# Roots from ScalarE's logarithm and exponential, and GpSimd's digit products in two halves of the tokens, in an audio tower kernel

## The chip, the cores and the metric

One core of a Trainium2 chip runs the whole kernel. The metric is the device time of one execution in microseconds (us), as the median of several runs. PE is the matmul engine, DVE the vector engine, ACT the scalar engine, POOL GpSimd, SP the queue that issues the transfers.

## The reference

The input is 32 clips of 40,000 samples. Cut to what matters:

```python
frames = pad(x).reshape(32, 313, 128)
h = einsum('bfh,kh->bfk', frames, dct_basis)             # 313 tokens of 128 per clip
n = layernorm(h)                                         # (h - mean) / sqrt(var + 1e-5)
h = h + softmax(n @ n.T) @ n                             # attention within a clip
n = layernorm(h)
q = layernorm((n @ Wq.T + bq) per head of 64) * ln_g + ln_b   # 8 heads
s0, s1 = l2norm(q[:32]) @ l2norm(keys0).T, l2norm(q[32:]) @ l2norm(keys1).T
top 16 of s0 and of s1, top 16 of their 256 sums, softmax -> w, expert index fi
h = h + sum over heads and picks of gelu(n . expert_down[fi]) * w * expert_up[fi]
```

Four roots stand in it: one for each layernorm over a token (1 and 2), one for the layernorm of each head (3), and one for the norm of each half of a head (4). A fifth, for the norm of the keys, is taken once.

## The kernel before

Two clips make a pair; there are 16 pairs. The 626 tokens of a pair are cut into five tiles of 128 tokens, so there are 80 tiles. The kernel has no loop on the device: every engine's program is written out, in an order that the function `drive` gives and that is the same for all of them.

`drive` cuts the time of a tile into four steps p = 0 to 3 (a slot is (pair k, tile t, step p)). In a slot each engine does the work of several tiles, each in another stage: scores and the top 16 of tile n, candidates of tile n-1, softmax weights of n-2, digits and products (`hi`, `lo`, `alpha`, `beta`, `bw`) of n-3, the small matmuls ("quads", `QB<-bw,alpha`) of n-4, the output of n-5. Between these slots stands the front of the next pair, `front(k + 1, t, p)`: transform and first squares in slot 0, attention in slots 0 and 1, second squares and `hid` in slot 2, head projections and their squares in slots 2 and 3, the head roots at (3,3), their transposes and the scores of the next pair in slot 4. Each engine works through its own list in order, and waits at a semaphore where its list asks for it; so one late instruction holds everything behind it on its engine.

The roots were made in two parts. DVE made a seed from the bits of the number (`seed`, L928 and L929; for the two row roots L980 brings the mean square first), and POOL made three Newton steps of four instructions each (`newton`, L780). Root 1 of the next pair: seed in DVE's slot 0, step 2, inside the list of `max_index` instructions, Newton at POOL's front (0,2), used by ACT's `xns` (L627) there. Root 2: seed at DVE's front (2,1), Newton at POOL's front (2,0), used by ACT's `hid` (L654) at (2,1). Root 3: seed at DVE's front (3,3), Newton and then a chain for `std` and `stdin` on POOL, transposed by PE at (4,0) and copied by ACT (`stdT`, L679). Root 4: seed by `norms` in DVE's slot 0, step 2, Newton at the head of POOL's slot (1,0).

POOL's products `bw` of a tile are three instructions (L914), each the product of `beta` with one of three parts of `wp`, for all 32 tokens of each group of the layout. PE's four steps of quads take the tokens 8 at a time: step p reads columns 8p to 8p+7. All four wait, by the wait at p = 0, for the whole of `bw`.

Per pair ACT calls Gelu once (slot 4, L719) and Exp many times: for `E` (L640, attention), `zexp` (L689) and `wexp` (L693). All its other functions are Copy, Identity, Square and Relu.

Of the kernel before, what the change touches and what calls it, by code (L numbers as in the profile page):

```python
# [9 lines left out]
I32 = mybir.dt.int32  # L10
# [28 lines left out]
RSQRT_MAGIC = float(0x5F3759DF)  # L39
# [41 lines left out]
def build(nc, x, Wq, bq, ln_g, ln_b, keys0, keys1, down, up, ident_d, dct_d, indc_d, sel_d, row8_d, sel3_d, out):  # L81
# [4 lines left out]
    with ctx:  # L86
# [6 lines left out]
        def sem(name):  # L93
# [12 lines left out]
        c15 = sb("c15", [128, 80])  # L106
# [55 lines left out]
        y4 = sb("y4", [128, 80])  # L162
# [75 lines left out]
            kseed_full knewton kn_full kbT_full dT_full weights_ready x_full xT_copied ss1_full sv1 seed1_full  # L238
            newton1 xn_full xnT_copied e_full rden_full h2c_full ss2_full sv2 seed2_full newton2 h2_full
            hid_full hidTn_full sq_full v3_full seed3_full newton3 std_full stdT_full hidT_full  # L240
# [5 lines left out]
            wb_steps stat_full vt_full std_steps nrm_steps n2_steps seed4_full""".split()  # L246
# [128 lines left out]
        def _(pe):  # L375
# [119 lines left out]
            def slot(k, t, p):  # L495
# [87 lines left out]
        def _(act):  # L583
# [14 lines left out]

            def squares(dst, src, over, b, done):


                for c, (st, n) in enumerate(CH):
                    last = A(over[0:n, b, c, 0:D], src(c, n), ACT.Square, accum_out=dst[0:n, 3 * b + c:3 * b + c + 1])
                last.then_inc(done, 1)
                return last

            def front(j, t, p):
# [14 lines left out]
                if (t, p) == (0, 2):  # L622
                    act.wait_ge(s["newton1"], 12 * j + 12)
# [26 lines left out]
                if (t, p) == (2, 1):  # L650
                    act.wait_ge(s["newton2"], 12 * j + 12)
# [15 lines left out]
                if (t, p) in ((2, 3), (3, 1)):  # L667
# [3 lines left out]
                    A(statT[:, NF * b:NF * b + NF], bank[0:40, 0:NF], ACT.Copy).then_inc(s["vt_full"], 1)  # L671
                if (t, p) == (4, 0):
# [10 lines left out]
            def slot(k, t, p):  # L683
# [10 lines left out]
                if p == 0 and exists(k, t, 3):  # L694
                    buf = RING[(t - 3) % NT]
                    act.wait_ge(s["st_full"], n - 2)
                    after(act, s["bw_full"], n - 4)
# [54 lines left out]
            def late(t, p):  # L752
                if (t, p) == (1, 3):
                    setup()
# [15 lines left out]
        def _(pool):  # L770
            tt = nc.gpsimd.tensor_tensor

            def newton(y, xh, a, c, sem_, base, end=None):

                i = 0
                for r in range(3):
                    for o, p0, p1, op in ((a, y, y, ALU.mult), (a, a, xh, ALU.mult), (a, a, c, ALU.add), (end if end is not None and r == 2 else y, y, a, ALU.mult)):
                        if i:
                            pool.wait_ge(sem_, base + i)
                        tt(o, p0, p1, op).then_inc(sem_, 1)  # L780
                        i += 1

            def setup():
# [3 lines left out]
                nc.gpsimd.memset(c15[:], 1.5)  # L787
# [13 lines left out]
            def late(t, p):  # L801
                if (t, p) == (0, 1):
                    pool.wait_ge(s["kseed_full"], 1)
                    newton(ky[:], kxh[:], ka[:], c15[0:64, 0:2], s["knewton"], 0)

            def front(j, t, p):
                if (t, p) == (0, 2):
                    pool.wait_ge(s["seed1_full"], j + 1)
                    newton(sy[0][:], sxh[0][:], sa[:, 0:6], c15[:, 0:6], s["newton1"], 12 * j)
                if (t, p) == (2, 0):  # L810
                    pool.wait_ge(s["seed2_full"], j + 1)
                    newton(sy[1][:], sxh[1][:], sa[:, 0:6], c15[:, 0:6], s["newton2"], 12 * j)
                if (t, p) == (3, 3):
                    pool.wait_ge(s["seed3_full"], j + 1)
                    newton(y3[:], xh3[:], sa[:], c15[:, 0:40], s["newton3"], 12 * j)
                    pool.wait_ge(s["newton3"], 12 * j + 12)
# [22 lines left out]
            def half_norms(j):  # L839
# [6 lines left out]

                tt(halves(nB[:]), halves(nB[:]), both(std[:]), ALU.mult).then_inc(s["nrm_steps"], 1)
# [18 lines left out]
            def slot(k, t, p):  # L866
# [10 lines left out]
                if p == 0 and t == 1 and exists(k, t, 0):  # L877
                    pool.wait_ge(s["seed4_full"], k + 1)
                    newton(y4[:], xh4[:], na[:], c15[:], s["rn_steps"], 12 * k, rn[:])
                if p == 0 and exists(k, t, 1):  # L880
# [3 lines left out]
                    pool.wait_ge(s["rn_steps"], 12 * kk + 12)  # L884
# [23 lines left out]
                if p == 3 and exists(k, t, 3):  # L908
# [14 lines left out]
        def _(dve):  # L923
            V = nc.vector

            def seed(x_, xh, y, done):

                V.tensor_scalar(xh, x_, -0.5, None, ALU.mult)  # L928
                V.tensor_scalar(y.bitcast(I32), x_.bitcast(I32), -0.5, RSQRT_MAGIC, ALU.mult, ALU.add).then_inc(done, 1)  # L929

# [3 lines left out]
            def setup():  # L934
# [8 lines left out]
                dve.wait_ge(s["kss_part"], 3)  # L943
                seed(kss[:], kxh[:], ky[:], s["kseed_full"])
# [258 lines left out]
```

## Time and profile before

| | |
|---|---|
| median of 3 runs | 2025.39 us (2025.3 to 2026.98) |
| the profiled execution | 2031.43 us, its span 2029.6 us |
| mean granted PE clock | 0.812 |
| busy in the span: PE, DVE, ACT, POOL | 1632.5, 1919.0, 1232.0, 1433.2 us |
| first and last tile begin on DVE (first L1062 of the tile) | 82.0 and 1945.0 us |

The rows further down come from the trace of the profiled execution. A row of a timeline says when a group of like instructions began, how long it took, what it wrote and read, and in square brackets how long the engine had been idle before it and what ended that. A row of the groups gives the busy time in all and the mean of one in ns. DMA plays no part: its queues are nearly empty.

### The profile page before, as it was taken

To read this page: it belongs to the slowest core of one execution; us is meant where nothing else is said; L and a number is where in the kernel's file an instruction comes from. 1 tells how busy PE (TensorE), PEld (TensorE's weight loads), DVE (VectorE), ACT (ScalarE), POOL (GpSimd) and SP (SyncE) were. 2 spreads that over 40 slices of the span, in tenths; PEclk is the share of its full clock that TensorE was granted. 3 is DMA by queue.
4 is the path that set the end of the run, shared out by engine and by line. 5 is a ranking of instruction groups with operands and counts; after the bars stand their busy time and mean duration, and the time that the engine had idled before them with its cause. 6 is when DMAs were issued, how large, how long until landed. Compare 5 with 4: busy or idle time off the path is not lost.

```text
span 2029.6 us, 47236 instructions
## 1 busy us (share of the span) xinstructions
PE 1632.5 (80%) x11023; PEld 1169.5 (58%) x11023; DVE 1919.0 (95%) x15718; ACT 1232.0 (61%) x3883; POOL 1433.2 (71%) x2561
## 2 busy tenths in 40 slices
PE   5577888788888888888888788888878888986667
PEld 3235566566656655665666556656656565655456
DVE  2499999999999999999999999999999999999992
ACT  3346666666666666566556766656675665665554
POOL 2247777686777767777776777777687777767775
PEclk8877888888888787888888787888888888788765
DMA  1000000000000000000000000000000000000000
GB/s 44 7 10 4 19 7 13 13 7 19 7 19 9 13 13 6 19 7 19 7 6 22 6 19 7 19 7 7 19 9 20 7 19 7 6 13 9 7 6 11
DMA packets 46669, 24.87 MB, mean 12 GB/s; under 512 B 4827, under 2 KB 46116, under 8 KB 46390
## 3 DMA queue, kind: packets, MB, share of 16 engines
q1 hardware_dynamic: 46390, 21.85, 3.9%
q8 instruction: 89, 1.46, 0.3%
q14 instruction: 190, 1.56, 0.3%
HBM read 11.58 MB, written 10.26 MB: 11 GB/s over the span
## 4 chain that ended last, share of the span: by engine, by line
DVE 79%; PE 11%; ACT 5%; issue 4%; POOL 1%; SPq 1%; DMA 0%; DVEq 0%; ACTq 0%
DVE idx L1071 11%; DVE idx L1078 11%; DVE hrest L1065 10%; DVE alpha L1039 10%; DVE vals L1069 7%; DVE vals L1062 7%; DVE c L1109 5%; DVE crest L1103 5%; DVE top L1106 3%; DVE top L1100 3%; PE QB L526 2%; DVE beta L1044 2%; PE FB L418 1%; PE QB L514 1%; DVE lo L1033 1%
## 5 line engine op out<-in xcount | busy, mean ns | idle before, releaser
L914 POOL TENSOR_TENSOR bw<-beta,wp 128x1024 bf16<-128x1024 bf16 x240 | 505.2, 2135 | 347.3 <-issue 171.6
L526 PE MATMUL QB<-bw,alpha 128*128 128x48 bf16 x5120 | 554.5, 277 | 106.7 <-issue 101.1
L526 PEld LDWEIGHTS QB<-bw,alpha 128*128 128x128 bf16 x5120 | 521.0, 150 | 149.2 <-issue 139.4
L749 ACT ACTIVATE WD<-QB 32x96 f32<-32x96 f32 x1280 | 307.6, 240 | 84.5 <-PE QB L526 71.6
L1039 DVE TENSOR_SCALAR alpha<-hi 128x1024 bf16<-128x1024 bf16 x640 | 274.9, 502 | 0.0
L475 PE MATMUL SC<-WK,hidT 128*128 128x512 f32 x320 | 241.0, 846 | 12.6 <-issue 11.8
L1071 DVE FIND_INDEX8 idx<-vals,sraw 128x8 uint32<-128x64 f32 x1280 | 250.6, 218 | 0.0
L1078 DVE FIND_INDEX8 idx<-vals,hrest 128x8 uint32<-128x64 f32 x1280 | 250.6, 219 | 0.0
L1065 DVE MATCH_REPLACE8 hrest<-vals,sraw 128x64 f32<-128x64 f32 x1280 | 249.6, 207 | 0.0
L1062 DVE MAX8 vals<-sraw 128x8 f32<-128x64 f32 x1280 | 169.1, 207 | 14.1 <-ACT sraw L729 14.1
L1069 DVE MAX8 vals<-hrest 128x8 f32<-128x64 f32 x1280 | 166.6, 208 | 0.0
L729 ACT ACTIVATE sraw<-SC 128x1024 f32<-128x1024 f32 x80 | 83.3, 1041 | 115.5 <-PE SC L476 114.8
L429 PE MATMUL FB<-hidTn,WcT 128*128 128x313 f32 x256 | 113.6, 594 | 49.2 <-ACT sq L665 37.2
L862 POOL TENSOR_TENSOR ci<-idxf 128x64 f32<-128x64 f32 (+3 forms) x400 | 126.2, 362 | 12.6 <-ACT idxf L710 12.5
L862 POOL TENSOR_TENSOR cs<-vs 128x64 f32<-128x64 f32 (+3 forms) x400 | 125.1, 350 | 6.3
L475 PEld LDWEIGHTS SC<-WK,hidT 128*128 128x128 f32 x320 | 79.8, 270 | 82.4 <-issue 76.1
L715 ACT ACTIVATE hi<-EB,cdig 128x256 bf16<-128x256 f32 x320 | 124.3, 473 | 0.0
L1109 DVE MATCH_REPLACE8 c<-top,crest 128x54 f32<-128x54 f32 x640 | 122.6, 243 | 0.0
L1103 DVE MATCH_REPLACE8 crest<-top,cs 128x54 f32<-128x54 f32 x640 | 118.8, 198 | 0.0
L493 PE MATMUL U<-wp,minusb 128*128 128x256 bf16 x160 | 51.2, 320 | 82.2 <-ACT wp L732 82.2
L514 PE MATMUL QB<-upR,Gd 128*128 128x128 f32 x640 | 112.2, 331 | 4.5 <-issue 4.2
L906 POOL TENSOR_TENSOR Yw<-wz,m 128x432 f32<-128x432 f32 x80 | 107.5, 1344 | 6.3
(206 smaller groups left out, 3583.3 us busy)
## 6 DMA issues: line engine op xcount, KB each, us to landing
res<-h_scratch SPq DMA_DIRECT2D x80, 64.0 KB, 1.9
xin<-in_x SPq DMA_DIRECT2D x32, 128.0 KB
h_scratch<-h2n SPq DMA_DIRECT2D x32, 128.0 KB
out<-ofin SPq DMA_DIRECT2D x64, 64.0 KB, 1.5
h_scratch<-h2n SPq DMA_DIRECT2D x32, 28.5 KB
out<-ofin SPq DMA_DIRECT2D x16, 57.0 KB
xin<-in_x SPq DMA_DIRECT2D x32, 28.0 KB
xin<-in_x SPq DMA_DIRECT2D x32, 0.2 KB
```

The lines of the kernel that those rows point to most:

```text
L475: mm(SC[:, cols], hidT[:, t1, :], WK[:, cols], start=True, stop=False)
L526: last = mm(bank[:, 48 * u:48 * u + 48], alpha[:, buf, a, :, 8 * p + u], bwv[:, :, a, :, 8 * p + u], start=(a == 0), stop=(a == 1))
L749: last = A(WD[r, RING[(t - 4) % NT], :, 8 * p:8 * p + 8], blocks[r, :, :, g], ACT.Copy)
L862: last = tt(o, a0, a1, ALU.add)
L914: last = tt(bw[:, buf, NY * i:NY * i + NY, :], beta[:, buf, :, :], wp[:, buf, i, :].unsqueeze(1).to_broadcast([128, NY, 256]), ALU.mult)
L1039: last = V.tensor_scalar(a8[:, :, :, xx, :], h8, BASE + float(NY * xx), None, ALU.is_equal)
L1062: V.max(vals[:, buf, i, 0:8], raw[i]).then_inc(chain, 1)
L1065: V.match_replace(rest[i], vals[:, buf, i, 0:8], raw[i], -1e30).then_inc(chain, 1)
L1069: V.max(vals[:, buf, i, 8:16], rest[i]).then_inc(chain, 1)
L1071: V.max_index(idx[:, buf, i, 0:8], vals[:, buf, i, 0:8], raw[i]).then_inc(chain, 1)
L1078: last = V.max_index(idx[:, buf, i, 8:16], vals[:, buf, i, 8:16], rest[i])
L1109: V.match_replace(c2[:, :, h], top[:, h, 8:16], crest[:, h, :], PICKED).then_inc(chain if h < H - 1 else s["c2_full"], 1)
```

## The change

Each root becomes: ACT takes Ln of the number with a scale, then Exp of -0.5 times that (`guess`; it is near the inverse root, off by a known factor), and POOL makes one step (`step`, four instructions) that brings it to full precision. DVE makes no seeds. For the row roots ACT also writes `sv` with an Identity (`row_guess`). The guesses stand in ACT's list at front (0,0) between the squares and the copies to `hcs` (root 1), at front (2,0) between the squares and `h2n` (root 2), at front (3,3) (root 3), at slot (k,0,3) ahead of `ofin` and `WD` (root 4), and at late (0,3) for the keys. The keys' POOL step moves from late (0,1) to late (0,3).

The products `bw` become six instructions in two halves of the tokens, with a semaphore step after each half; PE waits for the first half at p = 0 and for the second at p = 2. The waits on `bw_full` elsewhere count in twos.

```diff
                     if p == 0:
                         pe.wait_ge(s["alpha_full"], n - 3)
-                        pe.wait_ge(s["bw_full"], n - 3)
+                        pe.wait_ge(s["bw_full"], 2 * (n - 4) + 1)
+                    if p == 2:
+                        pe.wait_ge(s["bw_full"], 2 * (n - 4) + 2)
...
+            def guess(p, x_, scale, bias, sem_, value):
+                A(p, x_, ACT.Ln, scale=scale, bias=bias).then_inc(sem_, 1)
+                act.wait_ge(sem_, value)
+                A(p, p, ACT.Exp, scale=-0.5).then_inc(sem_, 1)
+
+            def row_guess(i, j):
+                sem_ = s["guess1"] if i == 0 else s["guess2"]
+                act.wait_ge(s["ss1_full"] if i == 0 else s["ss2_full"], 2 * j + 2)
+                guess(sxh[i][:], ss[i][:], (2.0 * D) ** (2.0 / 3.0) / D, cmin[:, 1:2], sem_, 3 * j + 1)
+                A(sv[i][:], ss[i][:], ACT.Identity, bias=cmin[:, 0:1]).then_inc(sem_, 1)
...
                         squares(ss[0], lambda c, n: bank[0:n, 129 * c:129 * c + D], xns, b, s["ss1_full"])
+                    row_guess(0, j)
+                    for b in range(2):
+                        bank = f_wait(act, f"hc{b}", j)
...
                         squares(ss[1], lambda c, n: h2c[0:n, b, c, :], hid, b, s["ss2_full"])
+                    row_guess(1, j)
...
+                if (t, p) == (3, 3):
+                    act.wait_ge(s["v3_full"], j + 1)
+                    guess(xh3[:], v3[:], 2.0 ** (2.0 / 3.0), 0.0, s["guess3"], 2 * j + 1)
...
+                if p == 3 and t == 0 and exists(k, 0, 0):
+                    act.wait_ge(s["n2_steps"], 2 * k + 2)
+                    guess(xh4[:], n2[:], 2.0 ** (2.0 / 3.0), 0.0, s["guess4"], 2 * k + 1)
...
+                if (t, p) == (0, 3):
+                    act.wait_ge(s["kss_part"], 3)
+                    guess(kxh[:], kss[:], 2.0 ** (2.0 / 3.0), 0.0, s["kguess"], 1)
...
-            def newton(y, xh, a, c, sem_, base, end=None):
-
-                i = 0
-                for r in range(3):
-                    for o, p0, p1, op in ((a, y, y, ALU.mult), (a, a, xh, ALU.mult), (a, a, c, ALU.add), (end if end is not None and r == 2 else y, y, a, ALU.mult)):
+            def step(out_, x_, p, a, lead, sem_, base):
+
+                tt(a, p, p, ALU.mult).then_inc(sem_, 1)
+                pool.wait_ge(sem_, base + 1)
+                tt(a, a, x_, ALU.mult).then_inc(sem_, 1)
+                pool.wait_ge(sem_, base + 2)
+                tt(a, lead, a, ALU.subtract).then_inc(sem_, 1)
+                pool.wait_ge(sem_, base + 3)
+                tt(out_, p, a, ALU.mult).then_inc(sem_, 1)
...
                 if (t, p) == (2, 0):
-                    pool.wait_ge(s["seed2_full"], j + 1)
-                    newton(sy[1][:], sxh[1][:], sa[:, 0:6], c15[:, 0:6], s["newton2"], 12 * j)
+                    pool.wait_ge(s["guess2"], 3 * j + 3)
+                    step(sy[1][:], sv[1][:], sxh[1][:], sa[:, 0:6], crow[:], s["newton2"], 4 * j)
...
                     after(pool, s["quads_full"], 4 * (n - 4))
-                    for i in range(3):
-                        last = tt(bw[:, buf, NY * i:NY * i + NY, :], beta[:, buf, :, :],
-                                  wp[:, buf, i, :].unsqueeze(1).to_broadcast([128, NY, 256]), ALU.mult)
-                    last.then_inc(s["bw_full"], 1)
+                    for half in range(2):
+                        q = slice(16 * half, 16 * half + 16)
+                        for i in range(3):
+                            o = bw[:, buf, NY * i:NY * i + NY, :].rearrange("p y (r q) -> p y r q", q=NQ)
+                            b0 = beta[:, buf, :, :].rearrange("p y (r q) -> p y r q", q=NQ)
+                            w0 = wp[:, buf, i, :].rearrange("p (r q) -> p r q", q=NQ)[:, :, q]
+                            last = tt(o[:, :, :, q], b0[:, :, :, q], w0.unsqueeze(1).to_broadcast([128, NY, 8, 16]), ALU.mult)
+                        last.then_inc(s["bw_full"], 1)
...
-            def seed(x_, xh, y, done):
-
-                V.tensor_scalar(xh, x_, -0.5, None, ALU.mult)
-                V.tensor_scalar(y.bitcast(I32), x_.bitcast(I32), -0.5, RSQRT_MAGIC, ALU.mult, ALU.add).then_inc(done, 1)
...
-            def row_seed(i, j, done):
-
-                dve.wait_ge((s["ss1_full"], s["ss2_full"])[i], 2 * j + 2)
-                V.tensor_scalar(sv[i][:], ss[i][:], 1.0 / D, 1e-5, ALU.mult, ALU.add).then_inc((s["sv1"], s["sv2"])[i], 1)
-                dve.wait_ge((s["sv1"], s["sv2"])[i], j + 1)
-                seed(sv[i][:], sxh[i][:], sy[i][:], done)
```

## Rows read from the trace of the kernel before

**Rows 1.** The page: busy time of each engine, and the chain that ended last

```profile
PE 1632.5 (80%) x11023; PEld 1169.5 (58%) x11023; DVE 1919.0 (95%) x15718; ACT 1232.0 (61%) x3883; POOL 1433.2 (71%) x2561
...
DVE 79%; PE 11%; ACT 5%; issue 4%; POOL 1%; SPq 1%; DMA 0%; DVEq 0%; ACTq 0%
```

**Rows 2.** Windows: busy us of each engine over 71 tiles of the steady part

```profile
205.10:1901.10 1696.00, 1413.22 (x9680) 1016.61 (x9680) 1688.15 (x13910) 1074.48 (x3392) 1261.28 (x2233) 0.83 0.04 12
```

**Rows 3.** Waits of ACT in the same stretch: us in total, times, longest

```profile
ACT xns L627 <- POOL sy L780: 31.1, 11, 3.5
ACT zexp L689 <- DVE c L1109: 23.6, 13, 8.3
```

**Rows 4.** Timeline of DVE, pair 7 slot 0; and groups, root 3's seed

```profile
911.18 0.20 DVE L928 TENSOR_SCALAR xh<-n 128x80 f32<-128x80 f32 x1
...
911.77 0.08 DVE L1078 MATCH_VALUE_LOAD idx<-vals,hrest 128x8 f32 x1
...
L928 DVE TENSOR_SCALAR xh<-v 128x40 f32<-128x40 f32 x16 | 10.5, 653 | 0.0
```

**Rows 5.** Line L1039 (alpha): duration ns min/median/max

```profile
L1039 DVE TENSOR_SCALAR alpha<-hi x640: 405/419/1628, 149.5 to 2003.6; 128x1024 bf16<-128x1024 bf16 x160
```

**Rows 6.** Timeline of ACT, pair 6, slots 2 to 4

```profile
834.91 1.86 ACT L648 ACTIVATE h2n<-h2c,hcs 128x128 f32<-128x128 f32 x6
...
840.17 1.88 ACT L654 ACTIVATE hid<-h2c,sy 128x128 f32<-128x128 f32 x6
...
856.63 0.30 ACT L689 ACTIVATE zexp<-top 128x128 f32<-128x128 f32 x1
...
877.75 1.56 ACT L715 ACTIVATE hi<-EB,cdig 128x256 bf16<-128x256 f32 x4
879.33 1.28 ACT L719 ACT_TABLE_LOAD   x1
880.62 0.57 ACT L719 ACTIVATE E<-SC 128x480 f32<-128x480 f32 x1
...
884.01 0.59 ACT L679 ACTIVATE stdT<-FB 81x512 bf16<-81x512 f32 x1 [0.90 <-PE FB L452]
```

**Rows 7.** Timeline of DVE, pair 6, slot 3

```profile
856.98 0.28 DVE L1088 TENSOR_REDUCE zs<-zexp 128x8 f32<-128x128 f32 x1
```

**Rows 8.** Timeline of ACT, pair 7, slots 0 and 1

```profile
911.68 1.00 ACT L749 ACTIVATE WD<-QB 32x96 f32<-32x96 f32 x4 [0.74 <-PE QB L526]
915.23 1.87 ACT L627 ACTIVATE xns<-hcs,sy 128x128 f32<-128x128 f32 x6 [2.55 <-POOL sy L780]
...
921.09 0.52 ACT L640 ACTIVATE E<-FB,cneg 57x313 f32<-57x313 f32 x1 [0.36 <-PE FB L410]
923.24 0.31 ACT L689 ACTIVATE zexp<-top 128x128 f32<-128x128 f32 x1 [1.63 <-DVE c L1109]
...
926.80 1.00 ACT L749 ACTIVATE WD<-QB 32x96 f32<-32x96 f32 x4
...
930.24 0.52 ACT L640 ACTIVATE E<-FB,cneg 57x313 f32<-57x313 f32 x1 [0.70 <-PE FB L410]
```

**Rows 9.** Timeline of POOL, pair 7, slot 0

```profile
911.94 0.20 POOL L780 TENSOR_TENSOR sa<-sy 128x6 f32<-128x6 f32 x1 [0.89 <-DVE sy L929]
...
915.00 0.20 POOL L780 TENSOR_TENSOR sy<-sy,sa 128x6 f32<-128x6 f32 x1
918.64 6.29 POOL L914 TENSOR_TENSOR bw<-beta,wp 128x1024 bf16<-128x1024 bf16 x3 [3.45 <-issue]
```

**Rows 10.** Timeline of PE, pair 7, slot 1

```profile
925.03 1.73 PE L526 MATMUL QB<-bw,alpha 128*128 128x48 bf16 x16 [3.97 <-issue]
926.59 3.62 PE L410 MATMUL FB<-xT 128*128 128x313 f32 x6
```

**Rows 11.** Timeline of PE in the tail, after the last tile has begun

```profile
1985.31 1.74 PE L526 MATMUL QB<-bw,alpha 128*128 128x48 bf16 x16 [2.80 <-issue]
...
2011.22 4.83 PE L526 MATMUL QB<-bw,alpha 128*128 128x48 bf16 x48 [1.99 <-issue]
```

More of the change, by code:

```diff
@@ L105, in build @@
         cdig = sb("cdig", [128, NS])
-        c15 = sb("c15", [128, 80])
+        clead = sb("clead", [128, 80])
+        crow = sb("crow", [128, 6])
+        cmin = sb("cmin", [128, 2])
         WcT = sb("WcT", [128, 512])
@@ L622, in front @@
                 if (t, p) == (0, 2):
-                    act.wait_ge(s["newton1"], 12 * j + 12)
+                    act.wait_ge(s["newton1"], 4 * j + 4)
                     act.wait_ge(s["hcs_full"], 2 * j + 2)
@@ L650, in front @@
                 if (t, p) == (2, 1):
-                    act.wait_ge(s["newton2"], 12 * j + 12)
+                    act.wait_ge(s["newton2"], 4 * j + 4)
                     for b in range(2):
@@ L696, in slot @@
                     act.wait_ge(s["st_full"], n - 2)
-                    after(act, s["bw_full"], n - 4)
+                    after(act, s["bw_full"], 2 * (n - 4))
                     A(wp[:, buf, 0, :], U[:, 0:256], ACT.Copy).then_inc(s["w1_full"], 1)
@@ L786, in setup @@
                 nc.gpsimd.memset(ss[1][:], 1.0)
-                nc.gpsimd.memset(c15[:], 1.5)
+                nc.gpsimd.memset(clead[:], 1.5 * 2.0 ** (1.0 / 3.0))
+                nc.gpsimd.memset(crow[:], 1.5 * (2.0 * D) ** (1.0 / 3.0))
+                nc.gpsimd.memset(cmin[:, 0:1], D * 1e-5)
+                nc.gpsimd.memset(cmin[:, 1:2], 1e-5 * (2.0 * D) ** (2.0 / 3.0))
                 nc.gpsimd.memset(one[:], 1.0)
@@ L801, in late @@
             def late(t, p):
-                if (t, p) == (0, 1):
-                    pool.wait_ge(s["kseed_full"], 1)
-                    newton(ky[:], kxh[:], ka[:], c15[0:64, 0:2], s["knewton"], 0)
+                if (t, p) == (0, 3):
+                    pool.wait_ge(s["kss_part"], 3)
+                    pool.wait_ge(s["kguess"], 2)
+                    step(ky[:], kss[:], kxh[:], ka[:], clead[0:64, 0:2], s["knewton"], 0)
             def front(j, t, p):
                 if (t, p) == (0, 2):
-                    pool.wait_ge(s["seed1_full"], j + 1)
-                    newton(sy[0][:], sxh[0][:], sa[:, 0:6], c15[:, 0:6], s["newton1"], 12 * j)
+                    pool.wait_ge(s["guess1"], 3 * j + 3)
+                    step(sy[0][:], sv[0][:], sxh[0][:], sa[:, 0:6], crow[:], s["newton1"], 4 * j)
                 if (t, p) == (2, 0):
-                    pool.wait_ge(s["seed2_full"], j + 1)
-                    newton(sy[1][:], sxh[1][:], sa[:, 0:6], c15[:, 0:6], s["newton2"], 12 * j)
+                    pool.wait_ge(s["guess2"], 3 * j + 3)
+                    step(sy[1][:], sv[1][:], sxh[1][:], sa[:, 0:6], crow[:], s["newton2"], 4 * j)
                 if (t, p) == (3, 3):
-                    pool.wait_ge(s["seed3_full"], j + 1)
-                    newton(y3[:], xh3[:], sa[:], c15[:, 0:40], s["newton3"], 12 * j)
-                    pool.wait_ge(s["newton3"], 12 * j + 12)
+                    pool.wait_ge(s["v3_full"], j + 1)
+                    pool.wait_ge(s["guess3"], 2 * j + 2)
+                    step(y3[:], v3[:], xh3[:], sa[:], clead[:, 0:40], s["newton3"], 4 * j)
+                    pool.wait_ge(s["newton3"], 4 * j + 4)
                     tt(std[:], v3[:], y3[:], ALU.mult).then_inc(s["std_steps"], 1)
@@ L877, in slot @@
                 if p == 0 and t == 1 and exists(k, t, 0):
-                    pool.wait_ge(s["seed4_full"], k + 1)
-                    newton(y4[:], xh4[:], na[:], c15[:], s["rn_steps"], 12 * k, rn[:])
+                    pool.wait_ge(s["n2_steps"], 2 * k + 2)
+                    pool.wait_ge(s["guess4"], 2 * k + 2)
+                    step(rn[:], n2[:], xh4[:], na[:], clead[:], s["rn_steps"], 4 * k)
                 if p == 0 and exists(k, t, 1):
@@ L883, in slot @@
                     kk, t1 = (k, t - 1) if t else (k - 1, NT - 1)
[L884 removed]
+                    pool.wait_ge(s["rn_steps"], 4 * kk + 4)
                     after(pool, s["cs_full"], n - 1)
@@ L971, in setup @@
                                 ALU.mult).then_inc(s["weights_ready"], 1)
-                dve.wait_ge(s["knewton"], 12)
+                dve.wait_ge(s["knewton"], 4)
                 for i in range(4):
@@ L975, in setup @@
                                     ALU.mult).then_inc(s["kn_full"], 1)
-            def row_seed(i, j, done):
-                dve.wait_ge((s["ss1_full"], s["ss2_full"])[i], 2 * j + 2)
-                V.tensor_scalar(sv[i][:], ss[i][:], 1.0 / D, 1e-5, ALU.mult, ALU.add).then_inc((s["sv1"], s["sv2"])[i], 1)
-                dve.wait_ge((s["sv1"], s["sv2"])[i], j + 1)
-                seed(sv[i][:], sxh[i][:], sy[i][:], done)
             def front(j, t, p):
-                if (t, p) == (0, 1) and j == 0:
-                    row_seed(0, j, s["seed1_full"])
                 if (t, p) == (1, 3):
@@ L1009, in front @@
                                     Bc2[:].unsqueeze(1).to_broadcast([128, NT, 16]), ALU.add).then_inc(s["stat_full"], 1)
-                    dve.wait_ge(s["v3_full"], j + 1)
-                    seed(v3[:], xh3[:], y3[:], s["seed3_full"])
             def norms(j):
                 dve.wait_ge(s["nrm_steps"], 4 * j + 4)
-                after(dve, s["rn_steps"], 12 * j)
+                after(dve, s["rn_steps"], 4 * j)
                 V.scalar_tensor_tensor(out=n2[:], in0=nw[:], scalar=1e-7, in1=n2[:], op0=ALU.mult, op1=ALU.max
@@ L1023, in norms @@
                                        ).then_inc(s["n2_steps"], 1)
-                dve.wait_ge(s["n2_steps"], 2 * j + 2)
-                seed(n2[:], xh4[:], y4[:], s["seed4_full"])
             def digits(k, t):
@@ L1040, in digits @@
                     last.then_inc(s["alpha_full"], 1)
-                    after(dve, s["bw_full"], n - 4)
+                    after(dve, s["bw_full"], 2 * (n - 4))
                     dve.wait_ge(s["lo_full"], n - 2)
```

22 lines of the change are left out of this document (5 added, 17 removed).

## The prediction

> **What bounds the kernel now.** I read the page first. DVE is busy 95% of the span and fills 79% of the chain that ended last; ACT is busy 61% and POOL 71% [rows 1]. That says: take work from DVE, give it to ACT. Then the windows, because a mean over the span hides the start and the tail: over 71 tiles DVE works 1688 of 1696 us, so a tile costs 23.89 us and a pair (five tiles) 119.4 us, and DVE has 0.5 us of idle time in each [rows 2]. DVE is the bound there. Third, the timeline of ACT, to see how far behind DVE the other engines run. ACT and PE hand work to each other in strict order through the front of the next pair, and this chain is nearly as long as DVE's own: in pair 6 ACT's `zexp` of slot 3 ends at 856.93 and DVE's `zs`, which needs it, begins at 856.98 [rows 6, 7]. So two bounds stand side by side, DVE's list and the ACT-PE chain. What the change is worth depends on what it adds to the second. Last, ACT's waits, which show what the chain has in reserve: in the 71 tiles (14 pairs) it waits 31.1 us for the Newton steps before `xns` and 23.6 us for DVE before `zexp`, 2.2 and 1.7 us per pair [rows 3].
>
> **What DVE gains.** Seed 4 and seed 1 together stand between 911.18 and 911.77: 0.59 us per pair [rows 4]. Seed 2 is half of such a group: 0.35, my estimate from the same rows. Seed 3's first instruction takes 653 ns in the mean against 200 for its like in slot 0, since it meets POOL's `bw` [rows 4]; with its second I take 1.1. Sum 2.0 us per pair. The `alpha` instructions have a median of 419 ns and a longest of 1628 [rows 5]; some are stretched where POOL is late, and fewer Newton steps make POOL less late. That may give DVE 0 to 3 us more. The whole gain counts only as long as DVE is the bound.
>
> **What ACT gets.** Per pair four guesses: four Ln, four Exp, two Identity. No Ln is in the trace, so the first question is what loading its table costs. A load takes 1.28 us, and the next ACTIVATE starts 1.29 us after the load began; the load began 0.02 after the work before it had ended [rows 6]. So a switch costs 1.3 us of ACT, all of it in line.
>
> The Trainium skill (ScalarE: Activation LUTs, "What ACT_TABLE_LOAD costs") counts about 2.66 us for a switch, since a drain of 1.38 comes on top. By this trace there is no such drain. What it would make of the sum is the last rival.
>
> How many switches? The bounds are none and two per guess: Ln's table and then Exp's, each time. The trace has one switch to Gelu and one back per pair, and each load stands right before the first instruction that lacks its function; nothing shows a set with Ln and Exp together, and `zexp` and `E` keep whatever set Exp first got. I take two per guess, the dear bound, since a Ln that is met alone gives no cause to pick a set that holds Exp too. That is a choice, and the first rival is its other side.
>
> The small ACTIVATEs cost 0.2 each (a `WD` copy takes 1.00 for four [rows 8]). Guess 3 and 4 are 2 x 1.3 + 2 x 0.2 = 3.0 us each, guess 1 and 2 with the Identity 3.2. Per pair 12.4 us on ACT, 14 of 119.
>
> **What lies beside other work**, in ACT's order. *Guess 1* (slot 0, 3.2): all behind it moves: copies, `Gd`, `sraw`, `wp`, `WD`. The `WD` at 911.68 had waited 0.74, so its end goes from 912.68 to 915.1. Then `xns` had waited for three Newton steps until 915.23 [rows 8]. POOL's twelve instructions lasted from 911.94 to 915.20 and had first waited 0.89 for the seed [rows 9]; four instructions (1.1 us) from 911.05 end at 912.2. So `xns` starts at 915.1 instead of 915.23: guess 1 is hidden. *Guess 4* (slot 0, 3.0) has no such cover. The last `E` of clip 0 ends at 924.6 instead of 921.6; `zexp` had waited 1.63 for DVE and goes from 923.24 to 924.6, `WD` from 926.80 to 928.2, and the `E` of 930.24 comes, with PE's product between two of them, at about 931.0 [rows 8]. PE had stood 3.97 us for `bw` before 925.03 [rows 10], which the first half now shortens, so it doesn't add. Left over: 0.8. *Guess 2* (slot 2, 3.2): from 834.91 to 842 ACT works without a gap, and `hid` follows it, not the Newton steps [rows 6]. On `hid` hang its transposes, the projections, their squares, statistics, `zexp` of slot 3. All 3.2 count. *Guess 3* (before slot 4, 3.0): ahead of `zexp`, `hi`, Gelu and the copies `hidT` and `stdT`. `stdT` had waited 0.90 for POOL's chain [rows 6]; POOL saves eight of twelve steps there, so that wait goes. Left: 2.1.
>
> The chain grows by 0.8 + 3.2 + 2.1 = 6.1 us per pair, to about 125.5, and DVE, at 117.4 or less, waits for it, mostly at `zs` in slot 3 where nothing is in reserve [rows 6, 7]. Behind `zs` stand DVE's second maxima and indices, and for them `cs`, `lo`, `alpha` and `beta` wait. DVE's 2.0 us then buy nothing.
>
> **The halves of bw.** An instruction of 6 elements takes 0.20 and three of 1024 take 6.29 [rows 9], so about 0.2 + 0.00186 per element; 512 elements make 1.15 and six 6.9. The first half is ready 3.45 after the start, 2.8 earlier, the second 0.6 later. The runs are now of 16 elements; if that costs half as much again, the block is 9.6. Either is hidden: in the chain `bw` is not what is last (POOL has 29% idle [rows 1]). In the steady part the halves bring nothing beyond slot 1's wait above. In the tail there is no front, and PE stood 2.80 and 1.99 us before quads [rows 11], which the first half takes away: -4.8 us. At the start three roots are in line; each trades 2.2 us of Newton steps and about 0.9 of seeds and waits for a guess of 3: I take 0, with 5 us either way.
>
> **Sum**, against the profiled execution's 2031.4: 14 full pairs x 6.1 = +85, tail -5: 2111. The median of the runs shown lies 6 lower: 2105 us.
>
> **Rivals.** *One table for both* (chance 0.09). If Ln comes with a set that also has Exp, three of four guesses need no load and one load per pair falls on guess 1, where it is hidden. A guess is 0.4 to 0.6. The chain grows by 0.6 + 0.4 - 0.9, nothing, and with DVE at 117.4 the pair lies between 117.4 and 119.4: 1990 to 2020, I say 2008. For: it needs only another choice of set. Against: nothing in the rows.
> The Trainium skill (ScalarE: Activation LUTs, "Table sets: the hidden batching unit") says just this: ln and exp share natural_log_exp_and_others, one load. No row here can show it.
>
> *ACT has the room* (0.06), the other side with the loads in place. ACT has 39% idle [rows 1], and much of it is waiting for PE. If PE runs ahead while ACT loads tables, more than the 6.1 is absorbed and DVE stays the bound: 14 x -2.0 - 5 gives 1992. It decides as soon as the chain's growth is under zero; each absorbed us per pair is 14 us. Against: `hid` follows ACT's own list without a gap, and PE's work there waits on `hid`.
>
> *A dearer switch* (0.03): 1.38 us more for each of eight per pair with nothing left to hide them is 11 us per pair, 14 x 11 = 155: 2260. Against it stands the 0.02 us gap before the load and the 1.29 behind [rows 6].
>
> *The forecast* has the rest, 0.82. Its own range: the leftover per pair could be 3 (guess 4 hidden and PE catching 2 us) to 8, that is 2060 to 2135. The 8-in-10 range goes a little beyond: 2035 to 2140; outside lie the rivals. A difference of 0.2% (4 us) is about what a measurement tells from none. Faster: first rival mostly and second, 0.14; same 0.03; slower 0.83.
>
> **What would show it.** Right: some 160 table loads instead of 33, at `guess`'s lines 16 times each and more; ACT busy near 1440; DVE idle of 6 to 8 us per pair at `zs` (L1088), put down to `zexp`; the wait of `xns` for `sy` gone; no DVE wait for `sv`; PE's first quads in the tail 2 to 3 us sooner after `beta`. Wrong: few loads, or DVE still busy 99% of the steady stretch. If DVE waits elsewhere (`v` of root 3, `lo`), the chain is right and its last link is not.

## The result, and the profile after

The changed kernel takes 2127.39 us (median of 4 runs) beside 2026.18 us for the kernel before: ratio 1.0498, 95% interval 1.048 to 1.0516. It is 5% slower; the forecast was 2105 us with a range to 2140. Its profiled execution took 2127.1 us, with a span of 2125.3.

The page of the changed kernel, the lines that answer to [rows 1]:

```profile
PE 1616.2 (76%) x11023; PEld 1176.0 (55%) x11023; DVE 1905.4 (90%) x15556; ACT 1428.4 (67%) x4175; POOL 1348.3 (63%) x2284
...
PE 45%; ACT 36%; DVE 11%; issue 6%; POOL 1%; SPq 0%; ACTq 0%; DMA 0%; DVEq 0%; POOLq 0%
```

DVE still has the largest busy share, but its share of the chain that ended last fell from 79% to 11%, and ACT and PE fill 81%. The bound has changed hands. Busy shares alone (90% DVE, 67% ACT) would name the wrong engine.

To see where the 95.7 us of span came from I cut both traces where the first `vals<-sraw` of a tile begins on DVE. The windows view for the 14 pairs between the first and the last, first the kernel before, then the changed one (columns: window, length; busy us and instructions of PE, PEld (its weight loads), DVE, ACT, POOL; granted PE clock, DMA share, GB/s):

```profile
181.20:1854.20 1673.00, 1400.81 (x9601) 1007.83 (x9601) 1665.15 (x13721) 1072.34 (x3389) 1244.61 (x2213) 0.83 0.04 12
```

```profile
185.00:1952.70 1767.70, 1374.51 (x9589) 1006.76 (x9590) 1654.75 (x13581) 1240.62 (x3638) 1176.34 (x1975) 0.82 0.04 11
```

| part of the span | before | after | difference | forecast |
|---|---|---|---|---|
| up to the first tile | 82.0 | 88.3 | +6.3 | 0 |
| first pair | 99.2 | 96.7 | -2.5 | not given |
| 14 pairs | 1673.0 | 1767.7 | +94.7 (6.8 each) | +85 (6.1 each) |
| last pair, up to its last tile | 90.8 | 89.6 | -1.2 | not given |
| tail from the last tile's start | 84.6 | 83.0 | -1.6 | -5 |

Nearly all of it is in the steady part, 6.8 us per pair. ACT's busy time there grew by 168.3 us, 12.0 per pair (forecast 12.4). DVE's fell by 10.4 us, 0.7 per pair, where 2.0 was forecast.

The groups of ACT, changed kernel (count, then us in all and mean ns): the table loads. L602 is Ln, L604 the Exp behind it, L740 Gelu, L710 `zexp`.

```profile
L602 ACT ACT_TABLE_LOAD x65 | 83.4, 1283 | 1.2
L604 ACT ACT_TABLE_LOAD x65 | 83.4, 1283 | 1.2
L740 ACT ACT_TABLE_LOAD x16 | 20.5, 1283 | 0.3
L710 ACT ACT_TABLE_LOAD x16 | 20.5, 1283 | 0.3
L627 ACT ACT_TABLE_LOAD x1 | 1.3, 1283 | 6.8 <-PE FB L383 6.8
```

163 loads stand where there were 33: two for each of 65 guesses. A set is what one load gives ACT: behind the load for Exp, the copies, squares and Exps here need no other until Ln or Gelu asks for one. The timeline of ACT in a middle pair, slot 2 up to slot 4, answers to [rows 6]:

```profile
1128.13 1.28 ACT L602 ACT_TABLE_LOAD   x1
1129.43 0.30 ACT L602 ACTIVATE sxh<-ss,cmin 128x6 f32<-128x6 f32 x1
1129.75 1.28 ACT L604 ACT_TABLE_LOAD   x1
1131.04 0.21 ACT L604 ACTIVATE sxh<-sxh 128x6 f32<-128x6 f32 x1
1131.15 0.28 ACT L611 ACTIVATE sv<-ss,cmin 128x6 f32<-128x6 f32 x1
1131.34 1.85 ACT L666 ACTIVATE h2n<-h2c,hcs 128x128 f32<-128x128 f32 x6
...
1136.59 1.88 ACT L672 ACTIVATE hid<-h2c,sy 128x128 f32<-128x128 f32 x6
...
1152.91 0.30 ACT L710 ACTIVATE zexp<-top 128x128 f32<-128x128 f32 x1
...
1172.03 1.28 ACT L602 ACT_TABLE_LOAD   x1
...
1182.41 0.59 ACT L700 ACTIVATE stdT<-FB 81x512 bf16<-81x512 f32 x1
```

Between the squares and `h2n` ACT now spends 3.2 us; no row up to `hid` has a wait in brackets, so all of it goes into `hid`. The wait of 0.90 that `stdT` had is gone. DVE meets the delay where `zs` needs `zexp`. Here, in one of the longest of these waits, it is idle for 8.9 us, where [rows 7] had no idle time:

```profile
1153.24 0.28 DVE L1102 TENSOR_REDUCE zs<-zexp 128x8 f32<-128x128 f32 x1 [8.91 <-ACT zexp L710]
```

The waits of the changed kernel between 211 and 1997 us (us in all, times, longest), against [rows 3]: the wait of `xns` for `sy`, 31.1 us before, is in none of its rows.

```profile
DVE zs L1102 <- ACT zexp L710: 109.1, 36, 9.0
...
ACT zexp L710 <- DVE c L1123: 7.3, 1, 7.3
```

In the chain that ended last of the changed kernel, in order of time, the loads are links, ahead of the work that they delay. A piece of it:

```profile
1126.24 1.88 ACT hid L617 x12
1128.13 1.28 ACT L602
1129.75 1.28 ACT L604
1131.44 1.75 ACT h2n L666 x6
...
1136.59 1.88 ACT hid L672 x6
...
1140.36 4.51 PE FB L428 x8
```

### The profile page after: what moved, and what is told of

The parts are those of the page before. It is cut to its first block, busy times and chain, and to the rows that moved or that the text cites. A ratio compares the mean times of both kernels' runs of the same rounds, so it can differ in the third digit from the quotient of the medians.

```text
span 2125.3 us, 47232 instructions
## 1 busy us (share of the span) xinstructions
PE 1616.2 (76%) x11023; PEld 1176.0 (55%) x11023; DVE 1905.4 (90%) x15556; ACT 1428.4 (67%) x4175; POOL 1348.3 (63%) x2284
## 4 chain that ended last, share of the span: by engine, by line
PE 45%; ACT 36%; DVE 11%; issue 6%; POOL 1%; SPq 0%; ACTq 0%; DMA 0%; DVEq 0%; POOLq 0%
PE QB L527 12%; PE SC L474 6%; ACT WD L773 5%; ACT hi L736 5%; PE FB L417 4%; PE QB L513 4%; PE FB L428 4%; ACT L602 3%; PE FB L437 3%; PE FB L409 2%; PE U L485 2%; ACT Gd L725 2%; ACT wexp L714 2%; DVE idx L1087 2%; DVE idx L1092 2%
## 5 line engine op out<-in xcount | busy, mean ns | idle before, releaser
L953 POOL TENSOR_TENSOR bw<-beta,wp 128x512 bf16<-128x512 bf16 x480 | 535.9, 1152 | 422.8 <-ACT wp L759 327.1
L773 ACT ACTIVATE WD<-QB 32x96 f32<-32x96 f32 x1280 | 307.3, 240 | 78.2 <-PE QB L527 67.0
L1055 DVE TENSOR_SCALAR alpha<-hi 128x1024 bf16<-128x1024 bf16 x640 | 284.4, 516 | 0.0
L474 PE MATMUL SC<-WK,hidT 128*128 128x512 f32 x320 | 224.1, 791 | 49.6 <-ACT stdT L702 49.6
L492 PEld LDWEIGHTS U<-wp,minusb 128*128 128x128 bf16 x160 | 17.0, 106 | 270.3 <-ACT wp L756 224.7
L753 ACT ACTIVATE sraw<-SC 128x1024 f32<-128x1024 f32 x80 | 83.2, 1040 | 101.1 <-PE SC L475 100.3
L895 POOL TENSOR_TENSOR ci<-idxf 128x64 f32<-128x64 f32 (+3 forms) x400 | 125.1, 355 | 36.0 <-ACT idxf L731 35.7
L474 PEld LDWEIGHTS SC<-WK,hidT 128*128 128x128 f32 x320 | 73.2, 248 | 109.3 <-issue 51.7
L513 PE MATMUL QB<-upR,Gd 128*128 128x128 f32 x640 | 125.5, 359 | 5.7 <-issue 4.2
L513 PEld LDWEIGHTS QB<-upR,Gd 128*128 128x128 f32 x640 | 114.9, 266 | 11.8 <-issue 9.3
```

Of the source, the lines that this page charges most:

```text
L474: mm(SC[:, cols], hidT[:, t1, :], WK[:, cols], start=True, stop=False)
L513: mm(FO, Gd[:, y, :], upR[:, y, :], start=(y == 0), stop=False)
L773: last = A(WD[r, RING[(t - 4) % NT], :, 8 * p:8 * p + 8], blocks[r, :, :, g], ACT.Copy)
L895: last = tt(o, a0, a1, ALU.add)
L953: last = tt(o[:, :, :, q], b0[:, :, :, q], w0.unsqueeze(1).to_broadcast([128, NY, 8, 16]), ALU.mult)
L1055: last = V.tensor_scalar(a8[:, :, :, xx, :], h8, BASE + float(NY * xx), None, ALU.is_equal)
```

## The experiments

All kernels compute the whole reference. "us per pair" is the length of the 14 pairs by 14, cut as above.

| run | median us | ratio to before (95%) | us per pair | table loads |
|---|---|---|---|---|
| the changed kernel | 2127.39 | 1.0498 (1.048 to 1.0516) | 126.3 | 163 |
| e1_one_set | 1981.21 | 0.9764 (0.975 to 0.9777) | 116.6 | 33 |
| e2_one_set_whole | 1975.09 | 0.9736 (0.9723 to 0.975) | 116.3 | 33 |
| e3_roots_only | 2127.27 | 1.0484 (1.047 to 1.0499) | 126.2 | 163 |
| e4_halves_only | 2036.07 | 1.003 (1.0019 to 1.0041) | 120.1 | 33 |
| e5_loads_g1_g4 | 2059.65 | 1.0145 (1.013 to 1.0161) | 122.6 | 97 |
| e6_loads_g2_g3 | 2068.07 | 1.0187 (1.0171 to 1.0203) | 123.0 | 97 |
| e7_h2n_late | 2090.58 | 1.0295 (1.0279 to 1.0311) | 123.8 | 163 |
| e8_one_set_whole_h2n | 1955.90 | 0.9648 (0.9632 to 0.9664) | 115.3 | 33 |
| e9_keys_no_loads | 2119.49 | 1.0449 (1.0434 to 1.0465) | 126.5 | 161 |
| e10_norms_late | 1958.06 | 0.9666 (0.9652 to 0.968) | 115.4 | 33 |
| e11_before_loads_g1 | 2042.69 | 1.0067 (1.0051 to 1.0084) | 120.2 | 65 |
| e12_before_loads_g2 | 2059.80 | 1.0161 (1.0148 to 1.0175) | 121.4 | 65 |

The kernel before is at 119.5 us per pair with 33 loads, and ran at 2028.3 to 2029.7 us in the median on the chips of these runs.

### One table set for Ln and Exp, with and without the halves

The changed kernel, with the set loaded by name once at the start and once per pair after Gelu; everything else stays:

```diff
                     act.wait_ge(s["gelu_full"], k + 1)
+                    nc.scalar.preload_act_table_set("natural_log_exp_and_others")
...
+            nc.scalar.preload_act_table_set("natural_log_exp_and_others")
             drive(act, slot, front, late)
```

> The changed kernel, with one table set that serves Ln and Exp loaded by an explicit instruction at the start and once per pair after Gelu, so that no guess switches tables. 33 or 34 loads instead of 163. Theory (the loads lengthen the ACT-PE chain): the time falls from 2127 to 2008, at most 2030, DVE is the bound again at 117.4 to 119.5 us per pair, and the waits of DVE for zexp in slot 3 are gone. Rival A (the guesses' own instructions and their places in ACT's list do it): stays above 2060. Rival B (the halves of bw do it, by strided reads on POOL): stays at 2110 to 2130.

Measured: 1981.21 us, 2.4% faster than the kernel before. The 130 loads were 166.8 us of ACT, and without them the kernel is 146.2 us shorter. The loads are the whole of the loss, and more: without them the change is a gain of 48 us. Rivals A and B of the expectation are out. The page of this kernel:

```profile
PE 1608.8 (82%) x11023; PEld 1173.5 (59%) x11023; DVE 1871.2 (95%) x15556; ACT 1259.5 (64%) x4045; POOL 1326.2 (67%) x2284
...
PE 49%; ACT 28%; DVE 17%; issue 4%; POOL 1%; SPq 1%; ACTq 0%; DMA 0%; DVEq 0%; POOLq 0%
```

The expectation's 2008 us was too high by 27. The first tile begins at 71.5 us instead of 82.0, where little had been expected, and a pair is 3.0 us shorter than before, at 116.6 instead of 117.4 or more. DVE is busy for 1621.5 of the 1631.7 us of the 14 pairs, and its waits at `zs` have nearly gone (6.4 us between 210 and 1850), as expected; yet the chain that ended last runs mostly through PE and ACT. The two bounds stand side by side again, and this run alone doesn't say which of them sets the time.

The same kernel with `bw` as three whole instructions again, as in the kernel before:

> As the run with one table set, but bw whole again as before (three instructions, one semaphore step). Theory: the steady part is the same within 0.3 us per pair; the tail is 3 to 5 us longer than with halves, so 2012. Rival B: 20 us or more faster than with the halves.

Measured: 1975.09 us, 6.1 us faster than with the halves, where 3 to 5 us slower had been expected. Single runs of the two kernels overlap, so the size is uncertain. The profiled executions are 3.4 us apart: the tail is 84.6 us against 83.2, so the halves give 1.4 us there and lose 4.8 elsewhere, 3.8 of them in the 14 pairs. The first product of `norms` takes 244 ns here and 551 with the halves.

### One part of the change alone

The changed kernel with whole `bw` (roots only), and the kernel before with `bw` in halves:

> The changed kernel with bw whole again: the new roots alone, with their 130 loads. Theory: the chain is bound by ACT, PE no longer finds the first half ready before slot 1's quads, 0 to 1 us per pair more, and the tail 3 to 5 us longer: 2131 to 2145. Rival B: near 2000, since the halves were the loss.

> The kernel before with bw in two halves and nothing else. Theory: DVE stays the bound, steady part 0 to +0.3 us per pair, tail 3 to 5 us shorter: 2022, against 2026 before. Rival B: 2080 or more.

Measured: roots only 2127.27, the changed kernel's own time, where 4 to 18 us more had been expected; halves only 2036.07, 7 us slower than before, where 4 us less had been expected. The groups of DVE, kernel with the halves only: the seed of root 3, and the first product of `norms`:

```profile
L935 DVE TENSOR_SCALAR y<-v 128x40 int32<-128x40 int32 x16 | 17.0, 1066 | 0.0
...
L1023 DVE SCALAR_TENSOR_TENSOR n<-nw,n 128x80 f32<-128x80 f32 x16 | 9.5, 594 | 0.0
```

In the kernel before they took 672 and 255 ns. The six instructions keep POOL busy a little longer (`bw` at 6.7 us a tile instead of 6.3), and what stands beside DVE's small instructions is different: 14 of the 16 seeds are now stretched beside a `bw` where 4 were, and 15 of the 16 products of `norms` beside POOL's `Yw`, again where 4 were. These two groups take 11.7 us more, on an engine that had nothing to spare, and the 14 pairs are 8.4 us longer. PE's idle time before its quads did fall, from 106.7 to 18.2 us, and bought nothing. In the changed kernel the bound is elsewhere, and the halves make no difference in all (2127.39 against 2127.27).

### Half of the loads

From the kernel with one set, the loads are put back for two of the four guesses of a pair (`loads` is True for guesses 1 and 4, or for 2 and 3):

```diff
             def guess(p, x_, scale, bias, sem_, value, loads=False):
+                if loads:
+                    nc.scalar.preload_act_table_set("natural_log")
                 A(p, x_, ACT.Ln, scale=scale, bias=bias).then_inc(sem_, 1)
                 act.wait_ge(sem_, value)
+                if loads:
+                    nc.scalar.preload_act_table_set("natural_log_exp_and_others")
                 A(p, p, ACT.Exp, scale=-0.5).then_inc(sem_, 1)
```

> The kernel with one table set, with two explicit loads put back around the Ln of guess 1 and of guess 4 only (as the changed kernel has them): 60 loads more than with one set. Theory (a load costs only what ACT's waits there don't hide: guess 1 nothing, guess 4 0.8 us per pair): 0 to 1.5 us per pair over the run with one set, and 3 us at the start: 1995, between 1984 and 2005. Rival (every load costs its 1.28 us in line wherever it stands, 5.1 us per pair): about 2055.

> The kernel with one table set, with two explicit loads put back around the Ln of guess 2 and of guess 3 only. Theory (these stand where ACT's list leads straight on to what DVE waits for): nearly all of the loss, 8 to 9 us per pair over the run with one set: 2105, between 2085 and 2120. Rival (every load counts the same): about 2055, as its twin with guesses 1 and 4.

Measured: 2059.65 and 2068.07. My theory said that the two pairs of guesses differ by 110 us; they differ by 8. The rival, 2055 for both, is near. Windows of the 14 pairs, in the order one set, loads of 1 and 4, loads of 2 and 3:

```profile
168.20:1799.90 1631.70, 1369.98 (x9593) 1006.56 (x9595) 1621.45 (x13581) 1095.22 (x3528) 1155.39 (x1975) 0.85 0.04 12
```

```profile
169.00:1884.70 1715.70, 1414.18 (x9587) 1016.97 (x9588) 1663.17 (x13581) 1168.91 (x3582) 1156.99 (x1975) 0.81 0.04 12
```

```profile
171.90:1894.30 1722.40, 1389.10 (x9602) 1013.84 (x9600) 1658.99 (x13581) 1167.56 (x3585) 1164.57 (x1976) 0.82 0.04 12
```

Four loads are 5.1 us of ACT per pair. On top of the kernel with one set they cost 6.0 us (1 and 4) or 6.5 us (2 and 3); as the last four of eight they cost 3.7 (2 and 3, the changed kernel less e5) or 3.2 (1 and 4, less e6). So the first loads cost more than their own length and the later ones less, wherever they stand. Part of the surplus is seen: the same instructions keep DVE busy 3.0 or 2.7 us longer per pair, and PE 3.2 or 1.4 us, with the granted clock at 0.81 and 0.82 in the mean instead of 0.85. Of DVE's part, 2.4 or 1.8 us are in the 40 `alpha` instructions of a pair, which take 534 and 521 ns in the mean instead of 475. Which of it lies on the chain these runs don't tell.

### Loads put into the kernel before

The rival reading of that miss was that placement never matters. The cover that the prediction counted (ACT waiting for the Newton steps) exists only in the kernel before, so two loads per pair were added to that kernel, behind the squares of the second clip at front (0,0), where guess 1 stands, or at front (2,0), where guess 2 stands:

```diff
                         squares(ss[0], lambda c, n: bank[0:n, 129 * c:129 * c + D], xns, b, s["ss1_full"])
+                        if b == 1:
+                            nc.scalar.preload_act_table_set("natural_log")
+                            nc.scalar.preload_act_table_set("exp_and_others")
```

> The kernel before, with two table loads put into ACT's list at front (0,0), behind the squares, where guess 1 stands in the changed kernel: 32 loads more, nothing else. Theory (the Newton steps of POOL keep xns waiting 2.2 us per pair there, so the loads are hidden): no change, 2022 to 2034 beside 2028. Rival (each load costs its 1.28 us): 38 us more, 2066.

> The kernel before, with two table loads at front (2,0), between the squares and h2n, where guess 2 stands. Theory (hid follows ACT's own list there; the chain of the kernel before has 1 to 2 us per pair left against DVE, so the rest of 2.6 counts): 0.6 to 1.6 us per pair, 2045. Rivals: hidden as at front (0,0), 2028; every load in full, 2066.

Measured: +14.4 us and +31.5 us over 2028.31, of 41.1 us of loads each. Both forecasts were too low: none had been expected of the first and 17 us of the second, which came out nearer to its rival (38). But here placement matters, as the prediction had it. The waits between 210 and 1850 us, first with the loads at root 1, then at root 2:

```profile
DVE sv L983 <- ACT hid L603: 17.1, 5, 4.9
...
ACT xns L630 <- POOL sy L783: 2.1, 4, 0.6
```

```profile
ACT xns L627 <- POOL sy L782: 30.2, 13, 3.0
DVE zs L1090 <- ACT zexp L691: 21.0, 14, 2.0
```

Loads at root 1 eat up the wait of `xns` (31.1 us in [rows 3], 2.1 here) and are paid only where that ends; DVE's waits there are five for the squares of root 2 (`sv`, 17.1 us, 2.3 in the kernel before); loads at root 2 leave it as it was and come out at DVE's `zs`.

### `h2n` moved, in the changed kernel and in the best one

Only stores to memory read `h2n`, and it stands ahead of `hid` on ACT. In both kernels its six instructions went from front (2,0) to front (2,3):

```diff
                     row_guess(1, j)
-                    for b in range(2):
-                        after(act, h2_stored[b], 32 * j)
-                        for c, (st, n) in enumerate(CH):
-                            last = A(h2n[0:n, b, c, :], h2c[0:n, b, c, :], ACT.Identity, bias=hcs[0:n, b, c, D:D + 1])
-                        last.then_inc(s["h2_full"], 1)
...
+                if (t, p) == (2, 3):
+                    for b in range(2):
...
                 if (t, p) in ((2, 3), (3, 1)):
```

> The changed kernel, with the six h2n instructions of ACT (1.85 us per pair) moved from between guess 2 and hid to front (2,3), ahead of the copy of the first statistics, where ACT waits 3 us for PE. Theory (the ACT-PE chain through guess 2 and hid is the bound): 1.9 us per pair off, 14 pairs, 2127 becomes 2101, between 2095 and 2110. Rival (DVE or the mean load of ACT is the bound; nothing is taken away, only moved): 2127.

> The fastest so far (one table set, bw whole, 1975) with the same move of h2n. Theory: there DVE's own list is nearly the bound (8 us of waits for zexp in 14 pairs), so at most 8 us come off: 1968 to 1975. Rival (the chain is still the bound): 26 us off, 1949.

Measured: 2090.58 (37 us less than the changed kernel, for 1.85 us of ACT moved per pair) and 1955.90 (19 us less than e2). In the first the work ahead of `hid` is paid in full and somewhat over, 2.5 us per pair for 1.85, where 1.9 had been expected; why it is more is not shown. The second is the best kernel of the study, 3.5% faster than the kernel before; it lies between the theory (at least 1968) and the rival (1949), so the chain counts there for more than had been expected.

### The keys' guess at the start

All loads as in the changed kernel, but none for the keys' guess, which stands between the Exps of the first attention:

> The changed kernel with the same loads around the Ln and Exp of guesses 1 to 4, but none for the keys' guess, which stands at the start between the Exp of the two clips' scores. In the changed kernel PE stood still there and its 36 matmuls of the attention output then took 10.8 us instead of 6.1 before. Theory (the keys' loads make a gap in PE's work, and PE then runs at half its clock): the first tile begins 7 us sooner, near 81 instead of 88.3 us; the 36 matmuls take 6 to 7 us; in all 2120. Rival (the loads cost their 2.6 us and the matmuls' length is chance): 2.6 us sooner and the matmuls stay at 10.8.

Measured: 2119.49, 7.9 us less; the first tile begins at 78.2 us instead of 88.3, and the pairs are 0.2 us longer. Timeline of PE at the start, changed kernel:

```profile
21.50 5.41 PE L409 MATMUL FB<-xT 128*128 128x313 f32 x10
29.23 1.04 PE L409 MATMUL FB<-xT 128*57 128x313 f32 x2 [2.32 <-ACT E L657]
30.20 10.89 PE L417 MATMUL FB<-xns,E 128*128 128x129 f32 x36
```

and without the keys' loads:

```profile
20.17 6.52 PE L409 MATMUL FB<-xT 128*128 128x313 f32 x12
26.63 6.17 PE L417 MATMUL FB<-xns,E 128*128 128x129 f32 x36
```

The same 36 matmuls take 10.89 us in the one and 6.17 in the other. The windows of the changed kernel (PE's granted clock is the third number from the end):

```profile
19.70:30.20 10.50, 8.16 (x19) 3.58 (x19) 1.93 (x6) 6.98 (x14) 0.75 (x4) 0.97 0.00 0
30.20:41.10 10.90, 10.90 (x38) 7.72 (x37) 1.50 (x8) 0.52 (x1) 0.00 (x0) 0.50 0.01 2
```

Over the block the granted clock is 0.50, half of full speed (1.2 of 2.4 GHz). The 0.97 ahead of it is too high for what PE did: the matmuls of L409 still take 728 ns and more at 25.1 us, the length that they have elsewhere at 0.50, and only at 26.2 us 427 ns, their length at 1.00. So PE had just come to full speed when it stood idle for 2.3 us, and behind that it was back at half. Without the loads it came to full speed at 25.9 us and kept it over the block. The other kernels agree: the three with loads at the keys' guess have an idle time of 2.3 to 2.6 us there and a block of 10.9 us, the eleven without have 0.1 us at most and 6.17.

Not all of the 10.1 us up to the first tile comes from the keys' loads. When the block of 36 ends the kernel is 8.3 us ahead, and 1.3 of these it had before the keys' guess already, since it loads its first set by name at 0.73 us.

### DVE's list shortened in the best kernel

`norms(k)`, whose second product meets POOL's `Ye` and takes 0.99 us, goes behind the second list of `max_index` instructions:

```diff
                             V.max_index(idx[:, buf, i, 0:8], vals[:, buf, i, 0:8], raw[i]).then_inc(chain, 1)
-                        if t == 0:
-                            norms(k)
                         for i in range(16):
...
+                        if t == 0:
+                            norms(k)
```

> The fastest so far (one table set, bw whole, h2n late, 1956), with DVE's two instructions of norms moved from the middle of its indices to behind them, 3 us later, where POOL has finished its products Ye. Theory (the second of them takes 1.02 us instead of 0.25 since POOL is at work, and DVE is the bound): it takes 0.25 to 0.3, 0.8 us per pair off, 1944. Rival (the ACT-PE chain is the bound, or whatever follows meets POOL in its place): 1956.

Measured: 1958.06, no gain. Windows of the 14 pairs, e8 and then this one:

```profile
164.40:1779.00 1614.60, 1387.15 (x9585) 1012.84 (x9583) 1601.11 (x13581) 1097.18 (x3525) 1124.77 (x1765) 0.83 0.05 13
```

```profile
164.60:1779.60 1615.00, 1385.65 (x9586) 1014.41 (x9586) 1591.45 (x13580) 1096.07 (x3527) 1125.39 (x1765) 0.83 0.05 13
```

DVE is busy 9.7 us less and the stretch is as long as it was, though DVE is busy for 99% of it in both. What it saved it waits at `zs` for `zexp`: 19.7 us in this stretch instead of 9.6. So the ACT-PE chain is the bound of the best kernel as well, and DVE has a little room beside it.

## Why the prediction was right, and where its terms were off

**How many switches: right.** Two per guess, 163 loads against "some 160". That was a choice between bounds which no row could decide, and it decided the sign: with one set the same change is 2.4% faster. The Trainium skill (ScalarE: Activation LUTs, "Table sets: the hidden batching unit") says that ln and exp lie in one set and need one load; e1 shows that this is so when the set is asked for by name, and the changed kernel shows that without the name it did not happen.

**What a switch costs: right.** 1283 ns in the mean, with the next ACTIVATE 0.01 to 0.02 us behind it. The Trainium skill (ScalarE: Activation LUTs, "What ACT_TABLE_LOAD costs") counts a drain of 1.38 us besides; no run here shows it. ACT's extra work was 12.0 us per pair, forecast 12.4.

**Which bound takes over, and where it is seen: right.** DVE waits at `zs`, 109.1 us in 71 tiles or 7.7 per pair (forecast 6 to 8), the waits of `xns` and `stdT` are gone, and DVE's savings buy nothing.

**The chain grows by 6.1 us per pair: 6.8 measured.** In the kernel before, each alone, e11 shows cover of about two thirds for loads at guess 1 (14.4 of 41.1 us count) where the prediction said all, and e12 shows three quarters in line for loads at guess 2 (31.5 of 41.1) where it said all. These two errors go against each other, so that the sum came near is in part luck. The single terms of the changed kernel can't be read off: e5 and e6 show that the price of a load depends on how many others are there. The sum was nearly right; that its terms add up was not shown, and by e5 and e6 they don't. Against the profiled execution the forecast of 2111 was 16 us short: 9.7 in the pairs, 6.3 at the start and 3.4 in the tail, less 3.7 in the first and last pair. The prediction then took off 6 us because the profiled execution before was that much above its median; that of the changed kernel was not.

**DVE gains 2.0 us per pair: 0.7 measured.** The seeds were worth more than that, 2.7 us. But the first product of `norms` (L1035) takes 787 ns where it took 255, since it now runs beside POOL's `Yw`, and `alpha` takes 516 ns in the mean instead of 502, 0.6 us per pair more, where the prediction had hoped for 0 to 3 less. It changed nothing in the time.

**The start, taken as 0: +6.3.** Root 1 was faster as thought (`xns` begins at 18.6 us instead of 24.5), but the prediction left the fifth guess out. The keys' two loads hold up an Exp that PE waits for, and PE's clock is half over the block behind it: 7.0 us together, which e9 gives back.

**The halves, -4.8 in the tail: -1.6.** The prediction took the waits of PE before its quads for what the tail would get back. They did go: behind the start of the last tile they came to 16.9 us in four before, and to one of 3.3 now. The quads of 1985.31, which had waited 2.80 [rows 11], are those of 2080.04 here: counted from the start of the last tile they begin 2.6 us sooner, with no wait. But further on in the same tile PE waits for ACT's `wp` instead, 15.1 us in the tail against 6.4. Timeline of PE, changed kernel:

```profile
2080.04 1.77 PE L527 MATMUL QB<-bw,alpha 128*128 128x48 bf16 x16
...
2086.74 0.39 PE L492 MATMUL U<-wp,minusb 128*128 128x256 bf16 x1 [3.18 <-ACT wp L756]
```

That `wp` stands behind `Gd` in ACT's list, and `Gd` waits for POOL's `G`, which stands behind the whole block of `bw`:

```profile
2085.01 1.26 ACT L725 ACTIVATE Gd<-G 32x128 f32<-32x128 f32 x4 [2.09 <-POOL G L909]
```

So the term failed at what follows: the first half comes sooner, and the end of the block, on which `G` hangs, does not. The kernel before with the halves alone has the same waits and the same tail (83.0 us).

The price of a product with runs of 16 was right: 1152 ns for 512 elements against an estimate of 1.15 us, 6.70 us a block against 6.9. What failed is "in the steady part the halves bring nothing": in the kernel before they cost 7 us, by all signs through DVE's small instructions (e4).

**The rival with one table set** was given 0.09 and 1990 to 2020 us. As a cure it exists, at 1981: below its range. It had counted DVE's savings in the steady part alone, 1 us per pair in the middle of its range, and nothing at the start. In fact a pair is 3.0 us shorter and the start 10.5. DVE's busy time fell by 3.1 us per pair, not by 2.0: the seeds 2.7, `alpha` 1.1 (475 ns instead of 502), less what `norms` and others lost. POOL has eight instructions less per root, for which ACT no longer waits. What share of the 3.0 us each has, no run separates.

## What to carry to other kernels

Before functions are moved to ACT, ask which table set each call would be given, count the loads in the trace, and name a common set by hand; here these two lines were worth 146 us. Take an engine's idle share for room only where the chain shows idle time in the place of the new work: cover such as a wait for another engine is spent once, and is gone when the same change removes that wait. Of work put into the list of an engine on the chain, look at what stands directly ahead of the next hand-over; moving six instructions that nobody waited for was worth 37 us and 19 us.

## What the runs showed of the hardware that was not expected

- At the start of the changed kernel PE had just come to full clock when it was idle for 2.3 us; it then ran a block of 36 matmuls at a granted clock of 0.50, in 10.89 us instead of 6.17. A delay of 2.3 us thus cost 7.0 (2.3 and the 4.7 between the two blocks).
- Four table loads (5.1 us of ACT) lengthened a pair by 6.0 and 6.5 us when they were the first, by 3.7 and 3.2 when they were the second four. DVE's and PE's busy times for the same instructions grew with them. How the surplus is made up stays open: in e9, with all the loads of the pairs, `alpha` takes 482 ns, nearly the 475 of e1, and a pair is as long as in the changed kernel.
- DVE instructions are longer beside POOL's: the first product of `norms` took from 255 to 787 ns, and the second 0.99 us beside POOL's `Ye` or 0.24 behind it. In the kernel before, the 557 `alpha` instructions with no POOL instruction beside them took 438 ns at most, the 83 others 1061 ns in the mean.
- In the changed kernel the pairs from the fifth on are alternately 127.6 or 127.5 and 125.1 us long. No run tells why.
